# Third layer's causal attention: scores and weighing of two head pairs interleaved on the TensorE array, with three and four buffers

## The chip, the cores and the metric

The kernel runs on one core of a Trainium2 chip. The metric is the device time of one execution in microseconds (us), the median of three runs. One execution was also profiled, and all rows below come from it.

## The reference

The program is a decoder of four layers on `x` of shape (16, 64, 256): 16 sequences of 64 tokens, 256 features, float32. The edit touches only the self-attention of the third layer (named L2, counted from 0):

```
x = x + L2_attn(layernorm(x))

q, k, v = h @ Wq + bq, h @ Wk + bk, h @ Wv + bv      # 16 heads of 16 features
scores  = q k^T / 4, masked above the diagonal        # 64 x 64 for each head and sequence
y       = softmax(scores) @ v
out     = y @ Wo + bo
```

## The kernel before

The program runs eleven stages one after the other: four attentions, three cross attentions, and the feed-forward parts, some merged. Each stage is one block with one instruction stream for each engine, and the engines meet on semaphores. Orders are written out by hand. `stage_L2_attn` is the sixth stage and begins some 683 us into the span.

Tokens lie as 8 tiles of 128 (two sequences each). The stage works on eight units u = 0 to 7, each of which is a pair of heads, so a unit has 32 of the 256 features. `c, i = divmod(u, 4)` gives the half of the features and the group of 32 rows in it. The eight PSUM banks are used so: scores of even units in banks 0 and 1, of odd units in 6 and 7; turned probabilities in 2 and 3; weighed values in 4 and 5.

For a unit TensorE does three things:

* `scores(u)`: two matmuls write the causal mask into two banks (L2533), then 16 small matmuls (L2536), one for each sequence, add query times key. They use 32 rows of the array (those of the unit) and 64 columns, and the 64-column group changes with each sequence. `kexp` holds each key twice with the other head of the pair set to zero, so one matmul gives 64 queries by 2 x 64 keys.
* `turn(u)`: eight 128 x 128 transposes of the probabilities (L2551).
* `weigh(u)`: 16 matmuls (L2561) of 128 rows and 32 columns, 64 tokens moving; all 16 go to the one group of 32 columns that belongs to the unit.

A float32 matmul shows as two records in the trace, so 16 of them are x32; a transpose shows as one.

VectorE does `centre(u)` (row maximum L2657, subtraction L2661) and `normalise(u)` (sum L2666, reciprocal L2668, product L2670), in the order centre 0, centre 1, normalise 0, centre 2, normalise 1, and so on to normalise 7. ScalarE does the exponential (L2626), then the two copies of an older unit's turned probabilities out of PSUM (`copy_turned`, L2608), and `copy_out` (L2612) when four units have been weighed. `pr` (scores to probabilities) and `pT` (turned) have two buffers each.

TensorE's order is: for u from 0 to 10, `scores(u)` if u is under 8, then from u = 2 `turn(u - 2)`, from u = 3 `weigh(u - 3)`. At u = 9 come the first four output products (L2568) ahead of the last turn. After the loop come the other output products, the addition to x (L2681) and the layer norm for the next stage.

`hold(k, bank, n)` (L1688) issues n matmuls of 128 x 512 bf16 whose result is not used; they keep TensorE busy where it would otherwise wait or work little.

Of the kernel before, what the change touches and what calls it, by code (L numbers as in the profile page):

```python
# [13 lines left out]
P = 128  # L14
# [1670 lines left out]
def hold(k, bank, n):  # L1685

    for _ in range(n):
        k.nc.tensor.matmul(k.ps[:, bank, :], k.ident16, k.causal, start=True, stop=True)  # L1688
# [787 lines left out]
def stage_L2_attn(k, w):  # L2476
# [6 lines left out]
    vblk = r.take(BATCH, 8, 2, 16)  # L2483
    bk = r.take(2, KC)
    yT = k.work.take(KC, TOK)
    pr, pT = k.work.take(2, 16, SEQ), k.work.take(2, NT, P)
    mx, sm, rs = k.work.take(2, 16), k.work.take(2, 16), k.work.take(2, 16)
    blank = k.work.take(D)
    with k.stage("bk", "qk", "queries", "keys", "xb", "v", "vzero", "vals", "scored", "maxed", "centred", "expd", "summed", "recip", "probs", "turned", "copied", "pv",
# [7 lines left out]
        @block.tensor  # L2497
        def _(pe):
            pe.wait_ge(w.sem, w.loaded)
            for i, t in enumerate((w.q, w.k)):  # L2500
                for m in range(2):
                    for half in range(2):
                        for c in range(KC):
                            last = nc.tensor.matmul(ps[:, 4 * i + 2 * m + half, :], t[:, c, m * P:(m + 1) * P],
                                                    k.hT[:, c, half * BANK:(half + 1) * BANK], start=c == 0, stop=c == KC - 1)
                    last.then_inc(s["qk"], 1)
            for b in range(BATCH):
                if b % 8 == 0:
                    pe.wait_ge(s["queries"], b // 8 + 1)
                for g in range(2):  # L2510
                    for c in range(KC):
                        last = nc.tensor.matmul(ps[64 * g:64 * g + 64, b // 4, (b % 4) * P:(b % 4 + 1) * P],
                                                k.hT[:, c, b * SEQ:(b + 1) * SEQ], w.v[:, c, g * P:(g + 1) * P],
                                                start=c == 0, stop=c == KC - 1, tile_position=(0, 64 * g))
                if b % 4 == 3:
                    last.then_inc(s["v"], 1)

            def scores(u):
                c, i = divmod(u, 4)
                at = 6 * (u % 2)  # L2520
                if u == 0:
                    pe.wait_ge(s["keys"], 2)
                    hold(k, 4, 5)
                    pe.wait_ge(s["vals"], 4)
                    pe.wait_ge(s["keys"], 4)
                elif u < 4:
                    hold(k, 5, (0, 0, 6, 3)[u])
                    pe.wait_ge(s["centred"], u - 1)
                elif u >= 2:
                    pe.wait_ge(s["centred"], u - 1)  # L2530
                rows = slice(32 * i, 32 * i + 32)
                for bank in range(2):
                    nc.tensor.matmul(ps[:, at + bank, :], k.ident16, k.causal, start=True, stop=False, skip_group_check=True)  # L2533
                for b in range(BATCH):
                    j = b // 2
                    last = nc.tensor.matmul(ps[64 * (b % 2):64 * (b % 2) + 64, at + j // 4, (j % 4) * P:(j % 4 + 1) * P],  # L2536
                                            qT[rows, c, b * SEQ:(b + 1) * SEQ], kexp[rows, c, :, b * SEQ:(b + 1) * SEQ],
                                            start=False, stop=True, skip_group_check=True, tile_position=(32 * i, 64 * (b % 2)))
                last.then_inc(s["scored"], 1)

            def turn(u):
                if u == 0:
                    hold(k, 5, 5)
                if u == 7:
                    pe.wait_ge(s["centred"], 8)
                    hold(k, 6, 8)
                pe.wait_ge(s["probs"], u + 1)
                if u:
                    pe.wait_ge(s["copied"], 2 * u)
                for j in range(NT):  # L2550
                    last = nc.tensor.transpose(ps[:, 2 + j // 4, (j % 4) * P:(j % 4 + 1) * P],  # L2551
                                               pr[:, u % 2, 2 * j:2 * j + 2, :].rearrange("p a t -> p (a t)"), k.ident)
                last.then_inc(s["turned"], 1)

            def weigh(u):
                c, i = divmod(u, 4)
                pe.wait_ge(s["copied"], 2 * u + 2)
                if c:
                    pe.wait_ge(s["yT"], 1)
                for b in range(BATCH):  # L2560
                    last = nc.tensor.matmul(ps[32 * i:32 * i + 32, 4 + b // 8, (b % 8) * SEQ:(b % 8 + 1) * SEQ],  # L2561
                                            vblk[:, b, u, :, :].rearrange("p g d -> p (g d)"),
                                            pT[:, u % 2, b // 2, 64 * (b % 2):64 * (b % 2) + 64], start=True, stop=True,
                                            tile_position=(0, 32 * i))
                last.then_inc(s["pv"], 1)

            def outputs(j, c):
                return nc.tensor.matmul(ps[:, j // 2, (j % 2) * D:(j % 2 + 1) * D], yT[:, c, j * P:(j + 1) * P], w.o[:, c, :],  # L2568
                                        start=c == 0 and j % 2 == 0, stop=c == KC - 1, skip_group_check=True)

            for u in range(8 + 3):
                if u < 8:
                    scores(u)
                if u == 9:
                    pe.wait_ge(s["yT"], 1)
                    pe.wait_ge(s["centred"], 7)
                    for j in range(4):
                        outputs(j, 0)
                if 2 <= u < 10:
                    turn(u - 2)  # L2580
                if u >= 3:
                    weigh(u - 3)
            pe.wait_ge(s["copied"], 16)
            for j in range(4, NT):
                outputs(j, 0)
            pe.wait_ge(s["yT"], KC)
            for j in range(NT):
                last = outputs(j, 1)
                if j % 2:
                    last.then_inc(s["out"], 1)  # L2590
            for i in range(NT // 2):
                hold(k, 6, (6, 3, 3, 1)[i])
                norm_turn(k, s, pe, i, (4, 5))
            hold(k, 6, 3)
# [6 lines left out]
            nc.gpsimd.memset(blank, 0.0).then_inc(s["blank"], 1)  # L2601

        def copy_turned(act, u):
            act.wait_ge(s["turned"], u + 1)
            if u >= 2:
                act.wait_ge(s["pv"], u - 1)
            for n in range(2):
                nc.scalar.copy(pT[:, u % 2, 4 * n:4 * n + 4, :].rearrange("p a b -> p (a b)"), ps[:, 2 + n, :]).then_inc(s["copied"], 1)  # L2608

        def copy_out(act, c):  # L2610
            act.wait_ge(s["pv"], 4 * c + 4)
# [3 lines left out]
        @block.scalar  # L2615
        def _(act):
            act.wait_ge(w.sem, w.loaded)
            act.wait_ge(s["bk"], 2)
            for m in range(2):
                act.wait_ge(s["qk"], m + 3)  # L2620
                for g in range(2):
                    nc.scalar.activation(kexp[:, m, g, :], ps[:, 4 + 2 * m:6 + 2 * m, :].rearrange("p a b -> p (a b)"), ACT.Identity,
                                         bias=bk[:, g, m:m + 1], scale=w.pmask[:, g:g + 1]).then_inc(s["keys"], 1)
            for u in range(8):
                act.wait_ge(s["centred"], u + 1)
                nc.scalar.activation(pr[:, u % 2, :, :], pr[:, u % 2, :, :], ACT.Exp, scale=0.25).then_inc(s["expd"], 1)  # L2626
                if u >= 2:
                    copy_turned(act, u - 2)
                if u == 6:
                    copy_out(act, 0)  # L2630
            copy_turned(act, 6)
            copy_turned(act, 7)
            copy_out(act, 1)
            norm_scalar_part(k, s, act, (4, 5))

        @block.vector
        def _(dve):
# [16 lines left out]
            def centre(u):  # L2654
                sc = ps[:, 6 * (u % 2):6 * (u % 2) + 2, :].rearrange("p a (h t) -> p (a h) t", t=SEQ)
                dve.wait_ge(s["scored"], u + 1)
                nc.vector.tensor_reduce(mx[:, u % 2, :], sc, AX.X, ALU.max).then_inc(s["maxed"], 1)  # L2657
                dve.wait_ge(s["maxed"], u + 1)
                if u >= 2:
                    dve.wait_ge(s["turned"], u - 1)  # L2660
                nc.vector.tensor_tensor(pr[:, u % 2, :, :], sc, bc(mx[:, u % 2, :], 2, SEQ), ALU.subtract).then_inc(s["centred"], 1)  # L2661

            def normalise(u):
                p, a, b = pr[:, u % 2, :, :], sm[:, u % 2, :], rs[:, u % 2, :]
                dve.wait_ge(s["expd"], u + 1)
                nc.vector.tensor_reduce(a, p, AX.X, ALU.add).then_inc(s["summed"], 1)  # L2666
                dve.wait_ge(s["summed"], u + 1)
# [927 lines left out]
```

## Time and profile before

| what | value |
|---|---|
| median of 3 runs | 1348.82 us (1344.62 to 1350.92) |
| the profiled execution's own time | 1344.42 us |
| its span, first to last instruction | 1342.7 us |
| mean granted TensorE clock | 0.993 |
| TensorE, VectorE, ScalarE busy share of the span | 93%, 59%, 44% |
| the changed loop (first mask to last weighing) | about 54 us |

The profile gives starts and durations in us from the span's start. A run of equal instructions is merged into one row, whose duration is that of the whole run; the distance between the starts of two neighbouring rows is what a run takes of its engine, and is a little less than the duration, because the end of the last matmul overlaps the start of the next. The arrow in brackets names what ended an idle time. PEclk is the granted TensorE clock; its two levels are 1.00 (2.4 GHz) and 0.50 (1.2 GHz).

### The profile page before, as it was taken

Reading aid. Unit: us, or ns where it says so; the run is one execution under the profiler, and the core shown is the slowest. Engines: PE = TensorE matmul, PEld = TensorE weight load, DVE = VectorE, ACT = ScalarE, POOL = GpSimd, SP = SyncE. Lnnn points to the kernel's source line nnn. Section 1 sums busy time; section 2 is a strip of 40 time slices with the busy share of each in tenths; the row PEclk is TensorE's granted clock in tenths of the full one; section 3 lists DMA queues with packets and bytes.
Section 4 is the critical chain, followed back from the end, with each engine's and each line's share of the span. In section 5 each row is a group of like instructions: output and inputs, shape, how many; then the busy total and the mean of one; then the engine's idle time right before and its main releaser. Section 6 shows DMA issues by size and latency. Waiting matters only on the chain. (4 is left out here: it accounts for less than half of the span.)

```text
span 1342.7 us, 30256 instructions
## 1 busy us (share of the span) xinstructions
PE 1245.0 (93%) x12658; PEld 932.8 (69%) x12658; DVE 798.1 (59%) x1511; ACT 591.1 (44%) x1070; POOL 378.9 (28%) x323
## 2 busy tenths in 40 slices
PE   6999998989999999999999889999997888999988
PEld 3479994559977677788867667888774445676545
DVE  5764566863363764633358665888644775873762
ACT  3632334684554674433433431232532453662751
POOL 0164303046630000555520005544102043532100
PEclk9999999999999999999999999999998999999999
DMA  4000004046024001000075080000016421211000
GB/s 125 4 2 4 4 4 127 1 109 131 1 68 146 2 2 36 1 0 1 1 165 166 1 264 1 1 1 2 2 71 199 133 61 47 55 30 33 2 1 32
DMA packets 81047, 68.36 MB, mean 51 GB/s; under 512 B 24968, under 2 KB 76880, under 8 KB 80784
## 3 DMA queue, kind: packets, MB, share of 16 engines
q1 hardware_dynamic: 78096, 63.63, 16.8%
q8 instruction: 101, 1.65, 0.5%
q0 software_dynamic: 768, 2.10, 0.5%
q10 hardware_dynamic: 2048, 0.70, 0.2%
q14 instruction: 34, 0.28, 0.1%
HBM read 53.82 MB, written 8.39 MB: 46 GB/s over the span
## 5 line engine op out<-in xcount | busy, mean ns | idle before, releaser
L1955 PE MATMUL ps<-rounded 128*128 128x512 f32 x384 | 91.2, 393 | 2.0 <-POOL rounded L1988 1.0
L1688 PE MATMUL ps<-fixed 128*128 128x512 bf16 x361 | 89.6, 389 | 1.9 <-PEq L78 1.9
L1342 POOL TENSOR_TENSOR fixed<-fixed,cross 128x768 f32<-128x768 f32 x32 | 58.9, 1839 | 104.5 <-DVE cross L1291 104.5
L1955 PEld LDWEIGHTS ps<-rounded 128*128 128x128 f32 x384 | 70.9, 188 | 20.3 <-POOL rounded L1988 5.3
L1256 PE MATMUL ps<-rounded 128*128 128x256 f32 x576 | 76.8, 287 | 1.3 <-DVE cross L1287 1.3
L1256 PEld LDWEIGHTS ps<-rounded 128*128 128x128 f32 x576 | 70.7, 190 | 5.4 <-issue 3.2
L1988 POOL TENSOR_TENSOR rounded<-weights,rounded 128x256 fp32r<-128x256 f32 x32 | 23.6, 760 | 179.7 <-ACT rounded L2006 179.7
L1321 ACT COPY cross<-ps 128x256 f32<-128x256 f32 x32 | 11.9, 372 | 112.9 <-PE ps L1265 112.9
L1688 PEld LDWEIGHTS ps<-fixed 128*128 128x128 bf16 x361 | 34.7, 99 | 37.8 <-issue 6.9
L2095 DVE TENSOR_TENSOR work<-work,ps 128x512 f32<-128x512 f32 x32 | 22.0, 687 | 62.0 <-ACT work L2023 59.9
L1629 POOL TENSOR_TENSOR work<-weights,work 64x512 f32<-64x512 f32 x32 | 41.2, 1287 | 54.3 <-DMA work<-work 33.5
L1265 PE MATMUL ps<-fixed,work 128*128 128x256 f32 x192 | 49.3, 393 | 7.4 <-POOL fixed L1342 7.0
L1876 DVE SCALAR_TENSOR_TENSOR fixed<-ps,work,fixed 128x256 f32<-128x256 f32 x64 | 27.7, 479 | 46.7 <-PE ps L1779 46.7
L227 PE MATMUL ps<-fixed 128*128 128x128 f32 x160 | 30.3, 303 | 20.8 <-ACT fixed L212 16.2
L525 DVE TENSOR_REDUCE work<-ps 128x16 f32<-128x1024 f32 x32 | 39.2, 1224 | 17.5 <-PE ps L373 16.9
L201 ACT ACTIVATE fixed<-fixed 128x2 f32<-128x2 f32 x48 | 13.6, 293 | 80.7 <-DVE fixed L173 80.6
L1805 POOL TENSOR_TENSOR rounded<-work,rounded 128x512 fp32r<-128x512 f32 x32 | 41.1, 1300 | 27.7 <-ACT rounded L1836 27.2
L1779 PE MATMUL ps<-rounded 128*128 128x256 f32 x384 | 47.9, 284 | 0.0
L1779 PEld LDWEIGHTS ps<-rounded 128*128 128x128 f32 x384 | 47.2, 192 | 1.0 <-POOL rounded L1805 0.4
L1974 PEld LDWEIGHTS ps<-rounded 128*128 128x128 f32 x384 | 47.0, 192 | 0.5
L1974 PE MATMUL ps<-rounded 128*128 128x256 f32 x384 | 47.2, 283 | 0.0
L1752 PE MATMUL ps<-rounded 128*128 128x512 f32 x192 | 45.8, 393 | 1.4 <-POOL rounded L1792 1.4
(497 smaller groups left out, 3056.0 us busy)
## 6 DMA issues: line engine op xcount, KB each, us to landing
weights<-in_L_ffn_masksT SPq DMA_DIRECT2D x32, 256.0 KB, 6.1
weights<-in_L_ffn_fc_w SPq DMA_DIRECT2D x16, 256.0 KB
weights<-in_L_xattn_Wq SPq DMA_DIRECT2D x2, 2048.0 KB, 10.1
weights<-in_L_xattn_WoT SPq DMA_DIRECT2D x2, 2048.0 KB, 11.1
work<-work SPq DMA_DIRECT2D x64, 64.0 KB, 2.0
sorted_in<-work SPq DMA_DIRECT2D x1, 3072.0 KB, 15.3
work<-sorted_in SPq DMA_DIRECT2D x12, 256.0 KB, 2.9
sorted_out<-work SPq DMA_DIRECT2D x12, 256.0 KB, 2.1
```

The costliest lines, as they stand in the source:

```text
L227: last = nc.tensor.transpose(k.ps[:, banks[i % 2], (2 * c + jj) * P:(2 * c + jj + 1) * P], k.h[:, 2 * i + jj, c * P:(c + 1) * P], k.ident)
L525: nc.vector.tensor_reduce(mx[:, j % 2, gp, :], ps[:, 0:2, :].rearrange("p a (n t) -> p (a n) t", t=SEQ), AX.X, ALU.max).then_inc(s["maxed" ...
L1256: last = nc.tensor.matmul(seen[:, a, :], m[:, u % 2, c, a, :], of[:, c, part * D:(part + 1) * D], start=c == 0 and n == 0, stop=c == KC - ...
L1265: last = nc.tensor.matmul(ps[:, 2, 0:D], c1[:, v // 4, a, :], ro[:, v % 2, a, :], start=a == 0, stop=a == 2)
L1342: nc.gpsimd.tensor_tensor(ro[:, v % 2, :, :], ro[:, v % 2, :, :], sn, ALU.add).then_inc(s["roped"], 1)
L1629: last = nc.gpsimd.tensor_tensor(qb[64:128, 2 * (u % 2) + e, tok], cs[made, v % 2, :], turned_sn[made, v % 2, :], ALU.add)
L1688: k.nc.tensor.matmul(k.ps[:, bank, :], k.ident16, k.causal, start=True, stop=True)
L1752: last = nc.tensor.matmul(ps[:, 2 * m + half, :], a[:, q % 2, c, :], b[:, c, half * BANK:(half + 1) * BANK], start=c == 0 and part == 0, s ...
L1779: last = nc.tensor.matmul(ps[:, 4 + i, jj * D:(jj + 1) * D], a[:, (e - 1) % 2, c, j * P:(j + 1) * P], b[:, (e - 1) % 2, c, :], start=c == ...
L1805: nc.gpsimd.tensor_tensor(a_rest[:, e % 2, m, tok], act1[:, (4 * e + 2 * m + half) % 3, :], a_top[:, e % 2, m, tok], ALU.subtract).then_in ...
L1955: last = nc.tensor.matmul(ps[:, 2 * (n % 2) + i, :], a[:, q % 2, i, c, :], b[:, c, half * BANK:(half + 1) * BANK], start=c == 0 and part = ...
L1974: last = nc.tensor.matmul(ps[:, 4 + i, jj * D:(jj + 1) * D], a[:, (e - 1) % 2, c, j * P:(j + 1) * P], b[:, (e - 1) % 2, c, :], start=c == ...
```

## The change

`scores(u)` is called for even u only and does units u and u + 1: four mask matmuls, then for each sequence one matmul of unit u and one of unit u + 1. The two units lie on neighbouring groups of 32 rows, so four tiles of the array follow each other. `weigh(u)` likewise does two units, alternating between two groups of 32 columns. Since scores of a pair of units wait for both earlier ones to be centred, TensorE waits for `centred` u instead of u - 1. `pr` gets three buffers, `pT` four. `turned` is now signalled for each half, so a copy starts after four transposes, and the next turn starts when the first copy is done. `copy_out(0)` moves behind the eighth exponential. The idle-filling matmuls change from 0, 6, 3 ahead of scores 1, 2, 3 to 14 ahead of scores 2.

```
-    pr, pT = k.work.take(2, 16, SEQ), k.work.take(2, NT, P)
+    pr, pT = k.work.take(3, 16, SEQ), k.work.take(4, NT, P)
...
-                elif u < 4:
-                    hold(k, 5, (0, 0, 6, 3)[u])
-                    pe.wait_ge(s["centred"], u - 1)
-                elif u >= 2:
-                    pe.wait_ge(s["centred"], u - 1)
-                rows = slice(32 * i, 32 * i + 32)
-                for bank in range(2):
-                    nc.tensor.matmul(ps[:, at + bank, :], k.ident16, k.causal, start=True, stop=False, skip_group_check=True)
+                else:
+                    if u == 2:
+                        hold(k, 5, 14)
+                    pe.wait_ge(s["centred"], u)
+                for at in (0, 1, 6, 7):
+                    nc.tensor.matmul(ps[:, at, :], k.ident16, k.causal, start=True, stop=False, skip_group_check=True)
                 for b in range(BATCH):
-                    j = b // 2
-                    last = nc.tensor.matmul(ps[64 * (b % 2):64 * (b % 2) + 64, at + j // 4, (j % 4) * P:(j % 4 + 1) * P],
-                                            qT[rows, c, b * SEQ:(b + 1) * SEQ], kexp[rows, c, :, b * SEQ:(b + 1) * SEQ],
-                                            start=False, stop=True, skip_group_check=True, tile_position=(32 * i, 64 * (b % 2)))
-                last.then_inc(s["scored"], 1)
+                    j, tok = b // 2, slice(b * SEQ, (b + 1) * SEQ)
+                    for n in (u, u + 1):
+                        c, i = divmod(n, 4)
+                        rows = slice(32 * i, 32 * i + 32)
+                        last = nc.tensor.matmul(ps[64 * (b % 2):64 * (b % 2) + 64, 6 * (n % 2) + j // 4, (j % 4) * P:(j % 4 + 1) * P],
+                                                qT[rows, c, tok], kexp[rows, c, :, tok],
+                                                start=False, stop=True, skip_group_check=True, tile_position=(32 * i, 64 * (b % 2)))
+                        if b == BATCH - 1:
+                            last.then_inc(s["scored"], 1)
...
             def turn(u):
...
-                if u:
-                    pe.wait_ge(s["copied"], 2 * u)
                 for j in range(NT):
+                    if u and j % 4 == 0:
+                        pe.wait_ge(s["copied"], 2 * u - 1 + j // 4)
...
             def weigh(u):
-                c, i = divmod(u, 4)
-                pe.wait_ge(s["copied"], 2 * u + 2)
-                if c:
+                pe.wait_ge(s["copied"], 2 * u + 4)
+                if u >= 4:
                     pe.wait_ge(s["yT"], 1)
                 for b in range(BATCH):
...
+                    for n in (u, u + 1):
+                        i = n % 4
+                        last = nc.tensor.matmul(ps[32 * i:32 * i + 32, 4 + b // 8, (b % 8) * SEQ:(b % 8 + 1) * SEQ],
+                                                vblk[:, b, n, :, :].rearrange("p g d -> p (g d)"),
+                                                pT[:, n % 4, b // 2, 64 * (b % 2):64 * (b % 2) + 64], start=True, stop=True,
+                                                tile_position=(0, 32 * i))
...
             for u in range(8 + 3):
-                if u < 8:
+                if u < 8 and u % 2 == 0:
                     scores(u)
...
-                if u >= 3:
-                    weigh(u - 3)
+                if u in (5, 7, 9):
+                    weigh(u - 5)
+            weigh(6)
...
         def copy_turned(act, u):
-            act.wait_ge(s["turned"], u + 1)
-            if u >= 2:
-                act.wait_ge(s["pv"], u - 1)
+            if u >= 4:
+                act.wait_ge(s["pv"], u - 3)
             for n in range(2):
-                nc.scalar.copy(pT[:, u % 2, 4 * n:4 * n + 4, :].rearrange("p a b -> p (a b)"), ps[:, 2 + n, :]).then_inc(s["copied"], 1)
+                act.wait_ge(s["turned"], 2 * u + n + 1)
+                nc.scalar.copy(pT[:, u % 4, 4 * n:4 * n + 4, :].rearrange("p a b -> p (a b)"), ps[:, 2 + n, :]).then_inc(s["copied"], 1)
...
-                if u == 6:
-                    copy_out(act, 0)
+            copy_out(act, 0)
             copy_turned(act, 6)
...
-                if u >= 2:
-                    dve.wait_ge(s["turned"], u - 1)
+                if u >= 3:
+                    dve.wait_ge(s["turned"], 2 * (u - 2))
```

## Rows read from the trace of the kernel before

**Rows 1.** The page's first line.

```profile
span 1342.7 us, 30256 instructions
```

**Rows 2.** Windows: length, busy us of each engine (instructions), clock, DMA share, GB/s.

```profile
724.00:746.00 22.00, 22.00 (x310) 18.59 (x308) 20.59 (x22) 9.19 (x14) 0.00 (x0) 1.00 0.01 2
746.00:762.50 16.50, 14.16 (x147) 11.95 (x145) 5.07 (x6) 6.45 (x9) 0.00 (x0) 1.00 0.00 1
```

**Rows 3.** Waits from 703 to 765 us: total, times, longest.

```profile
DVE work L2657 <- PE ps L2536: 3.8, 6, 2.6
...
DVE work L2661 <- PE ps L2551: 0.9, 1, 0.9
```

**Rows 4.** Timeline of TensorE: the first scores, and units in the steady stretch.

```profile
705.42 0.60 PE L2533 MATMUL ps<-fixed 128*128 128x512 bf16 x2 [0.30 <-DVE work L2650]
705.95 1.96 PE L2536 MATMUL ps<-work 32*64 32x128 f32 x32
...
730.65 1.96 PE L2536 MATMUL ps<-work 32*64 32x128 f32 x32
732.54 1.09 PE L2551 MATMUL ps<-fixed,work 128*128 128x128 f32 x8
733.56 1.97 PE L2561 MATMUL ps<-work 128*32 128x64 f32 x32
```

**Rows 5.** Timeline of VectorE: first maximum, one unit in full, last subtraction.

```profile
707.96 1.23 DVE L2657 TENSOR_REDUCE work<-ps 128x16 f32<-128x1024 f32 x1 [2.60 <-PE ps L2536]
...
732.66 1.22 DVE L2657 TENSOR_REDUCE work<-ps 128x16 f32<-128x1024 f32 x1 [0.20 <-PE ps L2536]
...
735.06 1.21 DVE L2666 TENSOR_REDUCE work<-work 128x16 f32<-128x1024 f32 x1
...
738.02 1.22 DVE L2657 TENSOR_REDUCE work<-ps 128x16 f32<-128x1024 f32 x1 [0.21 <-PE ps L2536]
...
744.63 1.22 DVE L2661 TENSOR_TENSOR work<-ps,work 128x1024 f32<-128x1024 f32 x1
```

**Rows 6.** Timeline of the stage's tail: TensorE, and VectorE's first addition.

```profile
748.59 1.09 PE L2551 MATMUL ps<-fixed,work 128*128 128x128 f32 x8 [2.33 <-DVE work L2670]
...
755.07 1.04 PE L2551 MATMUL ps<-fixed,work 128*128 128x128 f32 x8
756.04 3.57 PE L2561 MATMUL ps<-work 128*32 128x64 f32 x64
759.54 5.45 PE L2568 MATMUL ps<-weights,work 128*128 128x256 f32 x24
...
762.50 0.69 DVE L2681 TENSOR_TENSOR fixed<-fixed,ps 128x512 f32<-128x512 f32 x1 [11.29 <-PE ps L2568]
```

**Rows 7.** Timeline of small matmuls elsewhere; then L2536's durations, ns min/median/max.

```profile
495.15 1.10 PE L653 MATMUL ps<-weights,work 64*64 64x128 f32 x32
...
1141.16 1.15 PE L628 MATMUL ps<-work 128*64 128x64 f32 x32
...
L2536 PE MATMUL ps<-work x256: 267/268/471, 706.0 to 743.1; 32*64 32x128 f32 x128
```

**Rows 8.** Windows and TensorE's timeline where the granted clock was at its lower level.

```profile
710.00:713.60 3.60, 3.60 (x18) 1.11 (x12) 3.57 (x4) 1.75 (x2) 0.00 (x0) 0.58 1.07 345
...
1103.20 1.94 PE L1460 MATMUL ps<-fixed 128*128 128x128 f32 x8 [2.25 <-ACT fixed L1500]
...
1103.00:1106.50 3.50, 3.30 (x14) 2.86 (x15) 2.65 (x12) 2.21 (x9) 0.00 (x0) 0.51 0.09 20
...
1031.55 1.51 PE L2185 MATMUL ps<-fixed,work 128*128 128x128 f32 x6 [5.77 <-DMA work<-sorted_in]
```

**Rows 9.** Timeline of ScalarE around the end of the loop.

```profile
742.43 1.13 ACT L2612 ACTIVATE work<-ps,weights 128x1024 f32<-128x1024 f32 x1
745.89 1.06 ACT L2626 ACTIVATE work<-work 128x1024 f32<-128x1024 f32 x1 [2.33 <-DVE work L2661]
746.85 1.05 ACT L2608 COPY work<-ps 128x512 f32<-128x512 f32 x2
```

More of the change, by code:

```diff
@@ L2518, in scores @@
             def scores(u):
-                c, i = divmod(u, 4)
-                at = 6 * (u % 2)
                 if u == 0:
@@ L2547, in turn @@
                 pe.wait_ge(s["probs"], u + 1)
-                if u:
-                    pe.wait_ge(s["copied"], 2 * u)
                 for j in range(NT):
+                    if u and j % 4 == 0:
+                        pe.wait_ge(s["copied"], 2 * u - 1 + j // 4)
                     last = nc.tensor.transpose(ps[:, 2 + j // 4, (j % 4) * P:(j % 4 + 1) * P],
-                                               pr[:, u % 2, 2 * j:2 * j + 2, :].rearrange("p a t -> p (a t)"), k.ident)
-                last.then_inc(s["turned"], 1)
+                                               pr[:, u % 3, 2 * j:2 * j + 2, :].rearrange("p a t -> p (a t)"), k.ident)
+                    if j % 4 == 3:
+                        last.then_inc(s["turned"], 1)
             def weigh(u):
-                c, i = divmod(u, 4)
-                pe.wait_ge(s["copied"], 2 * u + 2)
-                if c:
+                pe.wait_ge(s["copied"], 2 * u + 4)
+                if u >= 4:
                     pe.wait_ge(s["yT"], 1)
                 for b in range(BATCH):
[L2561 to L2565, printed above, removed]
+                    for n in (u, u + 1):
[4 more added lines that the diff above has]
+                                                tile_position=(0, 32 * i))
+                        if b == BATCH - 1:
+                            last.then_inc(s["pv"], 1)
             def outputs(j, c):
@@ L2625, in _ @@
                 act.wait_ge(s["centred"], u + 1)
-                nc.scalar.activation(pr[:, u % 2, :, :], pr[:, u % 2, :, :], ACT.Exp, scale=0.25).then_inc(s["expd"], 1)
+                nc.scalar.activation(pr[:, u % 3, :, :], pr[:, u % 3, :, :], ACT.Exp, scale=0.25).then_inc(s["expd"], 1)
                 if u >= 2:
                     copy_turned(act, u - 2)
-                if u == 6:
-                    copy_out(act, 0)
+            copy_out(act, 0)
             copy_turned(act, 6)
@@ L2658, in centre @@
                 dve.wait_ge(s["maxed"], u + 1)
-                if u >= 2:
-                    dve.wait_ge(s["turned"], u - 1)
-                nc.vector.tensor_tensor(pr[:, u % 2, :, :], sc, bc(mx[:, u % 2, :], 2, SEQ), ALU.subtract).then_inc(s["centred"], 1)
+                if u >= 3:
+                    dve.wait_ge(s["turned"], 2 * (u - 2))
+                nc.vector.tensor_tensor(pr[:, u % 3, :, :], sc, bc(mx[:, u % 2, :], 2, SEQ), ALU.subtract).then_inc(s["centred"], 1)
             def normalise(u):
-                p, a, b = pr[:, u % 2, :, :], sm[:, u % 2, :], rs[:, u % 2, :]
+                p, a, b = pr[:, u % 3, :, :], sm[:, u % 2, :], rs[:, u % 2, :]
                 dve.wait_ge(s["expd"], u + 1)
```

## Prediction

> **What bounds the kernel now.** I read the page first: the span is 1342.7 us [rows 1], and the profiled execution's own time is 1344.42, so 1.7 us lie around the span. Then I looked for the stage in the windows. In the steady stretch TensorE is busy all 22.0 us and VectorE 20.59 of them [rows 2]. So TensorE sets the pace, but VectorE stands right behind it.
>
> The timelines say how closely. A unit takes TensorE, start to start, 1.89 us for the scores, 1.02 for the turn, and, with the two masks (0.53) and a weighing (1.91), 5.36 in all [rows 4]. VectorE's unit from maximum to maximum is the same 5.36 (732.66 to 738.02), of which it idled 0.21; a centring takes 2.40 (732.66 to 735.06), so a normalising takes 5.15 - 2.40 = 2.75 [rows 5]. Hence VectorE alone would need 5.15, and no speed of TensorE can bring a unit below that.
>
> The waits give what there is to win in the loop. VectorE waited 3.8 us for scores, 2.6 of it before the first, and 0.9 once for a turn [rows 3]; so 1.2 + 0.9 = 2.1 us between the first maximum (707.96) and the end of the last centring (744.63 + 1.22 = 745.85). Check: eight centrings and six normalisings are 19.2 + 16.5 = 35.7, plus 2.1 is 37.8; the rows give 37.89 [rows 5].
>
> Behind the loop TensorE bounds alone. From 745.85 it is 2.74 us to turn 6, which waits for VectorE; then come turn, weighing, output products, idle-filling matmuls, turn 7, and two weighings in a row, done at 759.54; 2.96 us later VectorE starts the first addition at 762.50 [rows 6].
>
> **The change part by part.**
>
> *Scores of two units.* Before: a run of 32 records takes 1.96 us [rows 4], of which the last record itself is 0.27 [rows 7], so the other 31 stand 54 ns apart. The nearest row for the new order is L653: 64 columns loaded, 128 moving, four tiles in turn, x32 in 1.10 us [rows 7]. With the same 0.27 for the last record that is 27 ns. 64 records then take 63 x 0.027 + 0.27 = 1.96 us, as long as one unit before. No row has 32 x 64 tiles on two row groups; the bounds are 1.96 and 3.85 (no gain from the row groups), and I take 1.96, since L653 differs only in rows.
>
> *Weighing of two units.* Before: 1.91 us start to start for 32 records, 60 ns each. The nearest row is L628 with 128 rows, 64 moving, two column groups in turn: x32 in 1.15 us [rows 7]. Two such runs back to back, 2.30 less one last record of some 0.25, are 2.05, and start to start somewhat less: 1.95, 30 ns a record. Bounds: 1.95 and 3.82 (twice 1.91). I take 1.95.
>
> One rule speaks against this. The Trainium skill ("TensorE: Matmul & The Clock Gate", Part 3, what overlaps and what doesn't) says that a weight load overlaps a matmul in flight only when the row group differs. Both weighed units use all 128 rows, so by it the pair would still take 3.8 us; the sum by that rule is a rival below. L628 uses all 128 rows too, and yet it ran at 30 ns: the trace speaks against the rule there.
>
> *Start of the loop.* Four masks instead of two (1.0 us) and 1.96 of scores put the first maximum at 705.42 + 1.0 + 1.96 + 0.05 = 708.4: 0.45 later.
>
> *Waits in the loop.* Scores 2k+2 now start only when centring 2k+1 is over. Then masks and scores take 1.0 + 1.96 + 0.1 of hand-over = 3.06, and VectorE has only normalising 2k, 2.75, to do meanwhile: 0.3 us of stall ahead of centrings 2 and 4. Ahead of centring 6 a weighing stands in front. From the end of normalising 3, TensorE does turn 3 (1.02), weigh 0 and 1 (1.95), masks, scores and hand-over (3.06): 6.03, where VectorE has centring 5 and normalising 4, 5.15: 0.9 us. In all 1.5 instead of 2.1. The third `pr` buffer takes away the 0.9 of L2661; it is in that 2.1. So the last centring ends 0.45 - 0.6 = 0.15 us earlier: the halved scores give almost nothing, because they were made to wait for the pair.
>
> *Tail.* After the end of the last centring: 2.74, turn 6 1.02, output products and idle-filling matmuls 3.55 (from turn 6 at 748.59 to turn 7 at 755.07 less a turn and a weighing), turn 7 0.97 [rows 6], two paired weighings 3.9 = 12.2. Before it was 759.54 - 745.85 = 13.7. Gain 1.5. Turns stay as they are.
>
> *ScalarE.* `copy_out(0)` moves behind exponential 7 and its copies: 1.06 + 1.05 + 1.13 = 3.2 us after the last centring [rows 9], and the output products that wait for it start at 2.74 + 1.02 = 3.76. It costs nothing, covered by 0.5 us. The copies per half and four `pT` buffers give nothing either: ScalarE is busy 9.19 of 22 us [rows 2]. The larger buffers only use room.
>
> *Clock.* TensorE's work falls, but the pace is VectorE's, so idle time appears. After the scores pair (3.06 from the centring's end) and a turn (1.0), the next turn waits until 0.3 + 2.75 + 2.40 + 2.75 = 8.2: a hole of 4.1 us, once for each pair, with no idle-filling matmuls in it. In the trace, 2.25 us of waiting ahead of 1103.20 was followed by a stretch at clock 0.51 to 1106.5, and the lower level also stood for most of 710 to 713.6, behind scores matmuls of 32 rows [rows 8]. A wait of 2.33 us at 748.59 went with a clock of 1.00 [rows 6, 2], so a hole of that size can go either way, but 4.1 is well above it. The stretch at half speed after the restart was 3.3 us long at 1103; it costs half of its length, 1.65, if all of it is on the path.
>
> The four holes: (a) before scores 2, some 1.8 us left by the 14 idle-filling matmuls (3.0 us at full clock): I take 0.3. (b) 3.1 us before turn 1 and 1.4 more before scores 4: part of the slow stretch meets masks and scores: 1.0. (c) 4.1 us before turn 3: the whole chain of 6.03 behind it is what VectorE waits for: 1.65. (d) 4.1 us before turn 5: that turn and a weighing, 2.97 at full and 4.6 at reduced speed, end 2.2 after the last centring, before turn 6 can start: 0. Tail, a hole of 2.2 at most as now: 0.3. Sum 3.25; bounds 0 and 7 (the whole of 1.65 at four places).
>
> **Sum:** -0.15 - 1.5 + 3.25 = +1.6 us. The span goes to 1344.3 and the own time to 1346.0. The median of the runs lies 4.4 above the profiled execution; on it the forecast is 1350.4.
>
> **The rivals.**
>
> *The clock stays up.* For it: the holes of 2.33 us passed. Against: 4.1 us is longer, and after 5.77 us of waiting [rows 8] TensorE restarted at half. Then -1.65: 1347.2. No rival goes much further: the loop can give at most the 2.1 us of stalls and the tail about 1.9, so faster by 0.5% (6.7 us, about what a measurement of this kernel can tell from no change) is out of reach except by scatter.
>
> *Tiles do not overlap as in the other stages.* If the paired weighing takes 3.82, the wait ahead of centring 6 grows by 1.9 and the tail by 3.7: +5.6 on the forecast, 1356.0. If the scores on two row groups take 3.85 instead of 1.96, the start and three centrings lose 1.9 each: +7.6, 1358.0. Against it both rows 7; for it that neither is the same shape. By the Trainium skill's rule on weight loads the weighing case holds: 1356.0.
>
> *Slower: the clock does not come back.* The pieces between the holes are themselves scores of 32 rows, behind which the clock fell at 710. Should it be at half from turn 1 to the end of the stage, masks and scores 4 lose 3.0, the chain before centring 6 6.0, and the tail (9.5 of work to the last weighing and 2.96 to the addition) 12.4: +21.4 - 1.65 = +19.8, 1368.6. It decides once more than 8.4 us of path work (at full speed) ran at half: 6.7 + 1.65. Against it: the slow stretches seen ended after some 3.3 us of work, and the tail has output products and idle-filling matmuls of full size.
>
> *The change does nothing to the time:* 1348.8; it can't be told from the first two.
>
> **How the numbers follow.** Forecast 0.52, clock stays up 0.25, tiles do not overlap 0.10, clock stays at half 0.07, anything else 0.06. The range takes in the first two cases with the scatter of the three runs (1344.6 to 1350.9), and the lower price of the third: 1343 to 1357. Beyond 0.5%: slower takes the fourth case, half of the third, and scatter, 0.10; faster only scatter, 0.03; within 0.5% 0.87.
>
> **What would show it.** L2536 as x64 in about 1.96 us and L2561 as x64 in about 2.1. VectorE's waits for L2536: three after the first, of about 0.3, 0.3 and 0.9 plus slow clock, none at L2661. TensorE idle some 4 us ahead of two turns, and windows behind them with a clock near 0.5. The first addition some 12.2 + 2.96 us after the last L2661. The prediction is wrong if 64 records take over 3 us, if the holes leave the clock at 1.00 (then 1347), or if it is at half in the tail.

## The result, and the profile after

The changed kernel takes 1354.53 us (median of 8 runs, 1351.42 to 1360.34) where the kernel before takes 1347.68 (8 runs, 1344.62 to 1350.92): a ratio of 1.0053, 95% interval 1.0035 to 1.0072. Measured again beside the experiments it was 1351.65 (12 runs), ratio 1.0018, interval 0.9992 to 1.0044. So the first measurement has it 0.5% slower; the second leans the same way, by 0.2%, but its interval takes in no change. The forecast was 1350.4 in a range of 1343 to 1357, with a chance of 0.87 on a difference within 0.5% and 0.10 on slower by more.

The first lines of the page, the granted clock in 40 slices among them:

```profile
span 1351.4 us, 30224 instructions
...
PE 1237.2 (92%) x12626; PEld 927.5 (69%) x12663; DVE 800.8 (59%) x1511; ACT 591.4 (44%) x1070; POOL 378.9 (28%) x323
...
PEclk9999999999999999999997899999998999999999
```

TensorE is busy for less time than before (1237.2 us; it was 1245.0) and the span is 8.7 us longer. The clock line already points at the place. The timeline of TensorE in the stage:

```profile
706.20 1.04 PE L2529 MATMUL ps<-fixed 128*128 128x512 bf16 x4 [0.30 <-DVE work L2653]
707.16 1.98 PE L2535 MATMUL ps<-work 32*64 32x128 f32 x64
...
718.08 1.04 PE L2551 MATMUL ps<-fixed,work 128*128 128x128 f32 x8
722.32 1.97 PE L2551 MATMUL ps<-fixed,work 128*128 128x128 f32 x8 [3.20 <-DVE work L2673]
724.72 1.89 PE L2529 MATMUL ps<-fixed 128*128 128x512 bf16 x4 [0.43 <-DVE work L2664]
726.54 3.69 PE L2535 MATMUL ps<-work 32*64 32x128 f32 x64
730.16 1.97 PE L2551 MATMUL ps<-fixed,work 128*128 128x128 f32 x8
735.49 1.97 PE L2551 MATMUL ps<-fixed,work 128*128 128x128 f32 x8 [3.36 <-DVE work L2673]
737.39 2.69 PE L2563 MATMUL ps<-work 128*32 128x64 f32 x64
...
748.21 1.97 PE L2551 MATMUL ps<-fixed,work 128*128 128x128 f32 x8 [4.23 <-DVE work L2673]
```

Read against [rows 4]: at 707.16 the scores of two units, 64 records, take 1.98 us, as long as 32 did. At 726.54 the same 64 take 3.69, masks 1.89 instead of 1.04, turns 1.97 instead of 1.09. Ahead of three turns stand holes of 3.20, 3.36 and 4.23 us.

The windows (length, busy us of each engine, then the clock as the third number from the end) show how long the lower level stood:

```profile
715.00:721.00 6.00, 3.96 (x77) 3.08 (x77) 5.48 (x7) 1.52 (x3) 0.00 (x0) 1.00 1.09 386
721.00:724.00 3.00, 1.68 (x8) 1.57 (x8) 2.93 (x4) 0.65 (x2) 0.00 (x0) 0.64 0.32 114
724.00:738.00 14.00, 10.21 (x98) 7.47 (x98) 10.85 (x12) 4.18 (x7) 0.00 (x0) 0.50 0.01 1
738.00:745.00 7.00, 5.82 (x133) 4.82 (x128) 4.40 (x5) 1.88 (x3) 0.00 (x0) 0.93 0.01 2
745.00:752.00 7.00, 3.79 (x44) 3.46 (x46) 6.83 (x8) 3.43 (x5) 0.00 (x0) 0.55 0.01 2
```

Some 17 us in one piece from 721 on, and 7 more from 745. Within the loop VectorE pays ahead of centrings 4 and 6 and nowhere else; the last line is the first addition behind it:

```profile
709.19 1.22 DVE L2660 TENSOR_REDUCE work<-ps 128x16 f32<-128x1024 f32 x1 [3.05 <-PE ps L2535]
...
717.11 1.23 DVE L2660 TENSOR_REDUCE work<-ps 128x16 f32<-128x1024 f32 x1 [0.38 <-PE ps L2535]
...
730.28 1.23 DVE L2660 TENSOR_REDUCE work<-ps 128x16 f32<-128x1024 f32 x1 [2.94 <-PE ps L2535]
...
743.00 1.23 DVE L2660 TENSOR_REDUCE work<-ps 128x16 f32<-128x1024 f32 x1 [2.50 <-PE ps L2535]
...
765.84 0.69 DVE L2684 TENSOR_TENSOR fixed<-fixed,ps 128x512 f32<-128x512 f32 x1 [9.94 <-PE ps L2571]
```

I call "stage time" the stretch from the first mask to the first addition: 765.84 - 706.20 = 59.64 us, against 762.50 - 705.42 = 57.08 before [rows 4, 6]. It divides into the time to the first maximum (2.99, was 2.54), the loop to the end of the last centring (41.37, was 37.89) and the tail (15.28, was 16.65). That is +2.56 us; the rest of the 8.7 lies in other stages, where the code is the same. Adding up windows of 1 us, the lower level stood for 13.7 us outside this stage in the trace before and 25.0 in the one after; in the ten further profiles below it was 18 to 41. So the profiled execution of before was a lucky one, and whole times are compared by many runs only.

### The profile page after: what moved, and what is told of

Same layout as the page of the kernel before. It is cut to its first block and busy times, and to the rows that moved or that the text cites. A ratio compares the mean times of both kernels' runs of the same rounds, so it can differ in the third digit from the quotient of the medians.

```text
span 1351.4 us, 30224 instructions
## 1 busy us (share of the span) xinstructions
PE 1237.2 (92%) x12626; PEld 927.5 (69%) x12663; DVE 800.8 (59%) x1511; ACT 591.4 (44%) x1070; POOL 378.9 (28%) x323
## 3 DMA queue, kind: packets, MB, share of 16 engines
q8 instruction: 101, 1.65, 0.5%
## 5 line engine op out<-in xcount | busy, mean ns | idle before, releaser
L1688 PE MATMUL ps<-fixed 128*128 128x512 bf16 x340 | 86.1, 392 | 4.3 <-PEq L78 2.0
```

## The experiments

Ten kernels ran, two of them repeats, with 5 rounds (12 runs) each and the kernel before on the same chip. Stage times and waits come from one profile each. A ratio below 1 is faster than before.

| kernel | stage, us | clock in it | waits ahead of centrings 2, 4, 6, us | ratio to before (95%) |
|---|---|---|---|---|
| before | 57.08 | 0.97 | 0.21, 0.38, 0.21 | 1 |
| changed | 59.64 | 0.80 | 0.38, 2.94, 2.50 | 1.0053 (1.0035 to 1.0072) |
| changed, again | 61.23 | 0.80 | 0.38, 2.94, 3.59 | 1.0018 (0.9992 to 1.0044) |
| changed, holes filled | 55.12 | 1.00 | 0.38, 0.38, 0.92 | 0.9968 (0.9945 to 0.9990) |
| changed, first holes filled | 58.68 | 0.88 | 0.38, 0.38, 3.61 | 1.0001 (0.9980 to 1.0021) |
| changed, without the 14 | 61.97 | 0.72 | 2.95, 2.68, 2.52 | 1.0058 (1.0037 to 1.0080) |
| scores paired only | 60.32 | 0.92 | 0.38, 3.51, 0.91 | 1.0025 (0.9996 to 1.0054) |
| weighing paired only | 57.66 | 0.82 | 0, 0, 2.73 (0.74 at 5) | 0.9992 (0.9963 to 1.0022) |
| buffers only | 58.17 | 0.94 | 0.21, 0.47, 0.20 | 1.0014 (0.9992 to 1.0035) |
| weighing paired, filled | 53.63 and 57.31 | 0.97 and 0.91 | 0, 0, 0.47 and 0, 1.14, 1.46 (1.68 at 5) | 0.9972 (0.9950 to 0.9994), 0.9973 (0.9957 to 0.9989) |
| the same, shorter tail | 51.96 | 0.97 | 0.21, 0, 0.47 | 0.9977 (0.9960 to 0.9994) |

**The changed kernel again.** Foreseen were 20 us or more at the lower level in the stage, 58 to 64 us for the stage and a whole 4 to 10 us slower than before; the rival was that the low clock of the first profile had been chance, with a stage of 55.5 to 56.5 us. The lower level stood for 23.9 us of the stage, as in the first profile, and the stage took 61.23, so the rival fell. The whole is 3.9 us slower by the medians, just under what was foreseen.

**Holes filled.** The first two lines stand in `scores(u)`, the others at the head of `turn(u)`.

```
+                    if u == 4:
+                        hold(k, 5, 5)
...
+                if u in (1, 3):
+                    hold(k, 5, {1: 12, 3: 17}[u])
+                if u == 5:
+                    for _ in range(17):
+                        nc.tensor.matmul(ps[64:128, 5, :], k.ident16[:, 0:64], k.causal, start=True, stop=True, tile_position=(0, 64))
```

> The changed kernel with idle-filling matmuls in its holes: 12 ahead of turn 1, 5 more ahead of scores 4, 17 ahead of turn 3, and ahead of turn 5 17 of half width (64 columns of the array) on rows of PSUM that the next weighing overwrites. Nothing else changes, and nothing of the result. Theory A (the changed kernel lost its time to the granted clock, which fell in the holes of 3 to 4 us): the clock stays at 1.00 from 715 us to the end of the stage, VectorE's waits for L2535-type scores fall from 8.9 us in all (3.05 of them the first) to about 4.6, the time from the first mask to the first addition of the stage falls from 59.6 us to about 55.4 (57.1 before the change), and the whole is 1 to 3 us faster than before the change, 7 to 9 faster than the changed kernel. Rival B (the time went to the pair of units waiting for each other, not to the clock): first mask to first addition stays at 58 us or more and the ratio to before stays at 1.003 or more. Rival C (17 idle-filling matmuls run over the end of the hole and delay the turn): the waits for scores ahead of centrings 4 and 6 stay above 2 us at full clock.

TensorE and VectorE in that kernel:

```profile
725.75 1.98 PE L2537 MATMUL ps<-work 32*64 32x128 f32 x64
727.66 1.09 PE L2558 MATMUL ps<-fixed,work 128*128 128x128 f32 x8
728.58 3.83 PE L1688 MATMUL ps<-fixed 128*128 128x512 bf16 x17
732.99 1.09 PE L2558 MATMUL ps<-fixed,work 128*128 128x128 f32 x8 [0.57 <-DVE work L2680]
734.01 1.98 PE L2570 MATMUL ps<-work 128*32 128x64 f32 x64
...
738.92 1.23 DVE L2667 TENSOR_REDUCE work<-ps 128x16 f32<-128x1024 f32 x1 [0.92 <-PE ps L2537]
...
706.25:761.37 55.12, 49.34 (x693) 34.11 (x694) 40.06 (x40) 19.79 (x27) 0.00 (x0) 1.00 0.30 99
```

All the difference to the changed kernel is work whose result nobody reads. The clock is 1.00 over the whole stage, the waits are 0.38, 0.38 and 0.92, and the stage is 4.5 and 6.1 us shorter than in the two profiles of the changed kernel. The whole is faster than before, by 0.1 to 0.55%. Theory A held; B and C fell.

**First holes filled only**, and **without the 14**, dose the same cause downwards and upwards. The first keeps, of the lines above, those for scores 4 and turn 1; the second takes out:

```
-                    if u == 2:
-                        hold(k, 5, 14)
```

> The changed kernel with idle-filling matmuls in its first holes only: 12 ahead of turn 1 and 5 ahead of scores 4; the holes ahead of turns 3 and 5 stay open. Theory A (each open hole costs by itself): the wait ahead of centring 4 falls from 2.94 us to 0.38, the clock is 1.00 until about 729 us and then falls in or behind the hole ahead of turn 3, where the wait ahead of centring 6 stays at 2 to 4 us; first mask to first addition 57 to 59 us, between the changed kernel (59.6 and 61.2) and the one with all holes filled (55.1); the whole half way between these two. Rival G (once the clock is kept up through the first hole it stays up): wait ahead of centring 6 of 0.92 and 55 to 55.5 us in all, as with all holes filled.

> The changed kernel without the 14 idle-filling matmuls ahead of scores 2: the opposite of filling, a hole of about 4.8 us there. Theory A: the clock falls already ahead of scores 2, VectorE waits 2 to 3.3 us ahead of centring 2 instead of 0.38, the rest as in the changed kernel, first mask to first addition 61 to 65 us, and the whole 2 to 3 us slower than the changed kernel (1.005 to 1.007 of before). Rival B (idle time of TensorE does not matter in itself): the same 59.6 to 61.2 us as the changed kernel, and a wait of 0.38 ahead of centring 2.

With the first holes filled, and then with none (windows as above):

```profile
715.00:727.00 12.00, 11.01 (x149) 7.07 (x142) 11.04 (x12) 4.03 (x6) 0.00 (x0) 1.00 0.55 197
727.00:733.00 6.00, 1.76 (x12) 1.53 (x11) 5.90 (x6) 2.02 (x3) 0.00 (x0) 0.83 0.00 0
733.00:740.00 7.00, 6.67 (x124) 5.69 (x127) 3.87 (x5) 2.02 (x3) 0.00 (x0) 0.66 0.01 2
```

```profile
711.00:715.00 4.00, 0.00 (x0) 0.13 (x2) 3.93 (x5) 1.29 (x2) 0.00 (x0) 0.53 1.03 314
715.00:721.00 6.00, 5.47 (x68) 3.88 (x69) 2.98 (x4) 0.82 (x1) 0.00 (x0) 0.50 1.09 387
```

The clock falls in the first hole left open and not before: at 727 to 733 in the one, at 711 in the other. Each centring behind an open hole waits some 2.5 to 3.6 us, each behind a filled one 0.38 or 0.92. Rival G fell. Without the 14 the whole is 1.0058 of before, as foreseen; that it is slower than the changed kernel by the 2 to 3 us expected is not shown, because that kernel measured 1.0053 and 1.0018.

**Scores paired only, weighing paired only.** The first keeps `weigh(u)` and the place of `copy_out(0)` of before; the second keeps `scores(u)` with its waits and idle-filling matmuls. Both have the new buffers.

> Only the scores are paired, with the 14 idle-filling matmuls, the buffers and the signals of the change; each unit is weighed by itself as before, and copy_out(0) is at its old place. Theory A: at full clock TensorE has 8.9 us of work in VectorE's 10.3 a pair, with one hole of about 2.2 us a pair ahead of turns 3 and 5 instead of 4.1; ahead of centrings 4 and 6 VectorE waits 0.85 each, so the loop is 0.4 us longer than before and the tail as before: first mask to first addition 57.5 us at full clock; up to 1.65 more for each of two holes if the clock falls in them, so 57.5 to 61, and the whole 0 to 4 us slower than before. Rival B (the pair's waiting is what costs): the same 58 to 60 but with the clock at 1.00. If the hole of 2.2 us keeps the clock and one of 4 us does not, the length of the hole is what counts.

> Only the weighing is paired, with the three and four buffers and the signals for each half; scores go unit by unit, with the waits and the idle-filling matmuls of before. Theory A (pairing the scores makes the holes that cost the clock; paired weighing by itself is cheap): TensorE needs 3.44 us a unit and 1.95 a pair of weighings, 8.8 of VectorE's 10.3, holes stay under 2 us, the clock is 1.00 from 724 us on, VectorE waits under 0.3 us between the first maximum and the last centring (2.1 before), first mask to first addition 53.5 to 54.5 us (57.1 before), the whole 2.5 to 4 us faster than before. Rival B (the late weighing and copy_out in the tail cost as much as the shorter weighing gives): first mask to first addition 56.5 or more. Rival D (any idle time of TensorE here brings the clock down): clock under 0.9 over 724 to 750 us and a time above that of before.

With the scores paired alone, VectorE waited 3.51 us behind the one hole of 3.20. The next hole, 2.33 us ahead of turn 3, left the clock at 1.00, and the wait was 0.91. Behind the third, 2.34 us ahead of turn 5, the clock fell: the weighing took 3.44 us instead of 1.97, where it delayed nothing:

```profile
721.47 1.97 PE L2551 MATMUL ps<-fixed,work 128*128 128x128 f32 x8 [3.20 <-DVE work L2671]
...
735.21 1.09 PE L2551 MATMUL ps<-fixed,work 128*128 128x128 f32 x8 [2.33 <-DVE work L2671]
...
735.00:740.00 5.00, 4.79 (x76) 3.87 (x80) 4.90 (x6) 2.02 (x3) 0.00 (x0) 1.00 0.01 3
...
746.34 1.09 PE L2551 MATMUL ps<-fixed,work 128*128 128x128 f32 x8 [2.34 <-DVE work L2671]
747.37 3.44 PE L2562 MATMUL ps<-work 128*32 128x64 f32 x32
```

So 2.3 us went either way within one profile, and the length of a hole alone does not decide. The weighing paired alone says so more plainly:

```profile
721.58 1.96 PE L2536 MATMUL ps<-work 32*64 32x128 f32 x32
725.19 1.24 PE L2551 MATMUL ps<-fixed,work 128*128 128x128 f32 x8 [1.65 <-DVE work L2673]
...
727.22 3.68 PE L2536 MATMUL ps<-work 32*64 32x128 f32 x32
...
732.72 3.63 PE L2563 MATMUL ps<-work 128*32 128x64 f32 x64
...
726.00:731.00 5.00, 5.00 (x38) 3.77 (x37) 4.15 (x6) 2.02 (x3) 0.00 (x0) 0.50 0.00 0
731.00:736.00 5.00, 5.00 (x70) 4.67 (x72) 4.90 (x5) 2.02 (x3) 0.00 (x0) 0.50 0.00 0
```

Here no hole was longer than 1.91 us, and yet the clock fell behind one of 1.65 that followed scores matmuls of 32 rows, and stayed down for some 10 us in which TensorE was busy without a break. Earlier in the same profile it fell with no hole at all, behind the first two scores:

```profile
706.00:709.00 3.00, 3.00 (x50) 2.40 (x46) 1.91 (x2) 0.00 (x0) 0.00 (x0) 0.99 1.08 355
709.00:712.00 3.00, 3.00 (x15) 1.29 (x11) 2.66 (x3) 1.06 (x1) 0.00 (x0) 0.50 1.00 298
```

TensorE was busy all of both stretches. So theory A was wrong here on the clock, the stage (57.66 us, foreseen 53.5 to 54.5) and the whole (0.9992, foreseen 2.5 to 4 us faster). D was right on the clock only: its time above that of before is not shown, and a hole of 0.29 us ahead of turn 1 left the clock at 1.00. Holes and few-row matmuls stand side by side in all these profiles, and no run takes them apart: which of the two brings the clock down, or whether it takes both, stays open.

**Buffers only.** Scores and weighing as before, three and four buffers, signals by halves.

> Only the buffers and signals of the change: three pr, four pT, the turn signalled by halves; scores and weighing unit by unit, all idle-filling matmuls and copy_out as before. Theory A (the buffers take away the one wait for a turned buffer and nothing else): no wait at the subtraction (0.89 before), the rest of the loop bound by TensorE at 5.36 us a unit, clock as before (a fall near 710 us, then 1.00), first mask to first addition 56.2 to 57.1 us against 57.1; the whole within 1 us of before. Rival H (buffers and half signals cost something in the changed kernel by themselves): 57.5 or more.

The wait at the subtraction is gone and the loop is 37.04 us, 0.85 less, as foreseen. The stage of 58.17 us misses theory A's 56.2 to 57.1 and lies where rival H had it (57.5 or more), but not for H's reason: the tail was 18.59 instead of 16.65: the hole ahead of turn 6, 2.33 us in this trace and in the one before [rows 6], cost the clock this time (turn 6 took 1.78 us). The whole, 1.0014, decides nothing: its interval takes in no change. The code around that hole is that of before except for the buffers and signals, so it is likely, though one profile of before does not show it, that the stage of before is itself not a fixed 57.08.

**Weighing paired, filled.** At the head of `turn(u)`:

```
+                if u in (2, 3):
+                    hold(k, 5, 6)
+                if u == 5:
+                    for _ in range(5):
+                        nc.tensor.matmul(ps[64:128, 5, :], k.ident16[:, 0:64], k.causal, start=True, stop=True, tile_position=(0, 64))
+                if u == 6:
+                    pe.wait_ge(s["centred"], 7)
+                    hold(k, 0, 8)
```

> The kernel with only the weighing paired, and idle-filling matmuls in its smaller holes: 6 ahead of turns 2 and 3, 5 of half width ahead of turn 5, 8 (after centring 7) ahead of turn 6. Theory A2 (paired small matmuls leave TensorE too little full work for the clock, whatever the length of a single hole; filling keeps it up and the freed time then shows): clock 1.00 from 714 us on, VectorE waits under 0.6 us between the first maximum and the last centring, first maximum to last centring 36.0 to 36.5 us (37.9 before), tail 15.0 (16.65 before), first mask to first addition 53.5 to 54.0 us against 57.1 before and 57.7 in the run without filling; the whole 4 to 7 us faster than before. Rival F (the wait for scores in the run without filling came from the order of turn, weighing and scores): VectorE still waits over 2 us ahead of centrings 6 or 7 at full clock, and the whole is as before.

> The kernel with paired weighing, single scores and filled holes once more, to narrow its interval. Theory A2: 0.995 to 0.999 of before; VectorE's wait in the loop 0.5 us or less; first mask to first addition 53.5 to 54 us. Rival: the first measurement was scatter, ratio 1.000.

The first profile has the stage as foreseen: one wait of 0.47 us in a loop of 36.18 (VectorE's own work is 35.7), 53.63 in all. In the second the clock fell after all, behind scores of 32 rows and 1.00 us of waiting ahead of turn 1, where I had filled nothing:

```profile
717.91 1.96 PE L2536 MATMUL ps<-work 32*64 32x128 f32 x32
720.87 1.65 PE L2559 MATMUL ps<-fixed,work 128*128 128x128 f32 x8 [1.00 <-DVE work L2681]
...
721.00:727.00 6.00, 6.00 (x43) 4.77 (x44) 4.78 (x5) 2.02 (x3) 0.00 (x0) 0.52 0.07 23
```

VectorE then waited 1.14, 1.68 and 1.46 us, where 0.5 at most was foreseen. Both measurements have the whole some 0.27% faster than before, so the first was no scatter, but that is less than the 4 to 7 us foreseen (3.0 and 3.3 by the medians), and the expected "clock of 1.00" is not a property of this kernel.

**Shorter tail:** the same without the 8 idle-filling matmuls ahead of turn 7.

> The same kernel without the 8 idle-filling matmuls ahead of turn 7, which stand on TensorE's path of the tail (probabilities 7 are ready before them). Theory P (the tail is TensorE's path alone, and its other work keeps the clock up): the tail from the last centring to the first addition falls from 14.9 to 13.2 us at a clock of 1.00, and the whole by 1.5 to 2 us against the kernel with them, 0.993 to 0.998 of before. Rival Q (the 8 are needed for the clock): tail 14.5 us or more with a clock under 0.95.

The tail (last centring to first addition) fell from 14.91 to 13.24 at a clock of 1.00, so in this profile they only stood in the way. The whole, 0.9977, cannot be told from 0.9973; 1.7 us is 0.12%, less than the interval.

**All runs together.** Each run also has its mean granted clock c, hence the time at the lower level, 2 (1 - c) times its span. A fit over all 221 runs of the twelve sets, with one base for each kernel and one slope for all, gives a slope of 0.35 us lost for each us at the lower level, with 1.5 us of scatter left:

```
                         runs   mean us   lower level us   base us (clock never down)
before                     93   1347.6        26.9           1338.2
changed (both sets)     8, 12   1355.0, 1352.1  51.1, 46.1   1337.1, 1336.0
changed, holes filled      12   1344.4        22.4           1336.5
changed, without the 14    12   1355.3        61.1           1333.8
scores paired only         12   1352.6        32.2           1341.4
weighing paired only       12   1348.0        40.2           1333.9
weighing paired, filled    12   1343.8        28.6           1333.8
```

By this fit, some 19 to 24 us more at the lower level cost the changed kernel 6.7 to 8.5 us. The bases are extrapolated and hold to 2 or 3 us at best: the kernel without the 14 gets 1333.8, and nothing in its edit could make it that much faster than the changed kernel at full clock. That the changed kernel's base lies 1 to 2 us below that of before is therefore not shown by the fit.

## Why the prediction was right, and where it was not

**Right at full clock, to 0.3 us.** With the holes filled the waits are 0.38, 0.38 and 0.92 where the sum had 0.3, 0.3 and 0.9; the time to the first maximum 3.00 (2.54 + 0.45); the loop 37.22 (35.7 + 1.5); from last centring to first addition 14.90 (12.2 + 2.96 = 15.16). In that last term two misses nearly cancel: the two paired weighings take 3.51 us instead of 3.9, and the addition starts 3.31 us after them instead of 2.96 (3.31 or 3.32 in every profile but that of before), which no run explains. The stage is 1.96 us shorter than before; the sum had 1.65. The interleaving itself does what it should: 64 records in 1.98 us for the scores, and in 1.98 for the weighing.

**The rule on weight loads.** The Trainium skill ("TensorE: Matmul & The Clock Gate", Part 3, what overlaps and what doesn't) lets a weight load overlap a matmul in flight only where the row group differs. The paired weighings both use all 128 rows and still run at 30 ns a record, half of the 60 before. The measurement decides against it for column groups.

**Right in direction on the clock.** Holes appear where the working put them: 3.20 (3.1 foreseen), then 3.36 and 4.23 (4.1), and the clock falls. Hole (d) was to cost nothing and the tail 0.3. In the first profile turn 6 starts 2.72 us after the last centring, as before; in the second 3.11, because the weighing ahead of it ran at the lower level throughout. In the first profile that weighing was slow in part and held up `copy_out(0)`, so the output products started 1.21 us after turn 6 instead of 0.93. The tail is 15.28 and 15.78 us against 14.90 with the holes filled, so (d) and the tail together cost 0.4 and 0.9. Hole (a) cost nothing either where I had 0.3, but it costs 2.6 if the 14 are taken away.

**Mis-sized: the length of the slow stretch.** This is the term of the sum that failed. It was 3.3 us at the lower level for each hole, restarted each time. What happened is one stretch of 17 us (722 to 739 in the first profile, 724 to 741 in the second) that bridged holes (b) and (c): the 7.4 us of work without a break between the holes did not bring the clock back. The prices: hole (b) 2.94 - 0.38 = 2.56 us in both profiles, where I had 1.0; hole (c) 2.50 - 0.92 = 1.6 and 2.7, where I had 1.65. With the tail these make up all of the 4.5 and 6.1 us by which the two profiles exceed the filled one; the sum had 3.25 for the clock. In the stage the forecast was +1.6; two profiles show +2.56 and +4.15. The rival "the clock does not come back" named such a stretch, but took it to last too long: the clock was at 1.00 again from 739 to 745, and from 753 through the rest of the tail. Its reason, the 32-row scores between the holes, no run separates from the others.

**What was luck.** The forecast put the kernel 1.6 us above the median of before; the medians have it 6.9 and 3.9 above. The range held because its upper end, 1357, came from another rival, tiles that do not overlap, which did not occur; the clock's price alone, at the size given it, would not have reached 1354.5. The chances were also added wrongly: the fourth case (0.07) and half of the third (0.05) are 0.12 already, where 0.10 was given to slower by more than 0.5%, and that is where the first measurement fell.

**Not foreseen: small holes are enough.** I priced holes by their length. Weighing paired alone lost the clock behind 1.65 us. The kernel before kept it from 724 to 746, where TensorE, its bottleneck, had no break [rows 2]; in each of the unfilled kernels in which TensorE got faster there, the clock fell in or behind one of the new holes. That unbroken work is what keeps it up is argued from this, and the kernels with filled holes speak for it; that it is not enough by itself is shown by the fall at 709 in the kernel with paired weighing.

**Open.** The changed kernel is 7.7 to 10.6 us slower than with its holes filled by the means of the runs, but the two profiles differ from the filled one by 4.5 and 6.1 in the stage. Only the 7.7 compares kernels measured together, and it has a standard error of 0.9 us, so the 1.6 us beyond 6.1 are not clear of noise; the 10.6 compares two measurements made apart. What remains was not located; where the clock falls in other stages varies from run to run, and one profile of each cannot settle it.

## What to carry to other kernels

Before speeding up TensorE in a loop, look at what comes next: if another engine has 96% of its period, as here 5.15 of 5.36 us, the freed time turns into holes, and the holes can cost the clock, and so more than was freed. Then put work into the holes in the same edit, ahead of each wait that the new bound makes, and check the granted clock by windows, not by the mean, and in more than one profile: at one place left open, ahead of turn 1, TensorE waited 0.23 us in one profile of a kernel and kept the clock, and waited 1.00 us in the other and lost it. Where the time of one kernel spreads by 1% with the clock, as here (1342.6 to 1358.4 for the kernel before), compare many runs, with their clocks beside them.

## What the runs showed of the hardware that was not expected

* Scores of 32 rows run at 30 ns a record, start to start, instead of 59 when two row groups take turns as well as two column groups (64 records in 1.98 us, 32 in 1.96 before).
* Matmuls whose result nobody reads kept the clock up: 17 of them in a hole of 4.4 us held it at 1.00, and so did 17 of 64 columns in the next one.
* The clock also fell with TensorE busy without a break: from 0.99 over 706 to 709 us to 0.50 over 709 to 712 in the kernel with paired weighing, behind two scores of 32 rows.
* Once down, the clock stayed down for 10 us of TensorE work without a break when that work was turns, scores and weighings (726 to 736 in the kernel with paired weighing).
* Holes of one length went either way: 2.33 us ahead of turn 6 kept the clock in the kernel before and lost it with the buffers only, and 2.33 and 2.34 us went one way each in the profile of the paired scores. The two profiles of the kernel with paired weighing and filled holes, with the same instructions, differ by 3.7 us in the stage. So a single profile is one draw.
